# The end of an attention kernel: unit-matrix sums of two steps at a time, and a last block without GpSimd

## What is computed

```python
tgt = concat([target (B,S,64), pos (B,S,2)]) @ proj_w + proj_b
din = concat([tgt, seq, tgt - seq, tgt * seq])          # 256 features
h = sigmoid(din @ w1 + b1)                               # 80 units
h = sigmoid(h @ w2 + b2)                                 # 40 units
score = where(mask == 0, -1e9, h @ w3 + b3)              # (B, S)
attn = softmax(score, axis=-1)
out = einsum('bs,bsd->bd', attn, seq)                    # (512, 64)
```

## Time and profile before

| | us |
|---|---|
| median of 3 runs (lowest, highest) | 285.75 (284.81, 287.69) |
| profiled execution | 287.8 |
| its span in the profile | 286.0 |

### The profile page before, as it was taken

The page is one execution under the profiler, slowest core; times in us unless marked ns, Lnnn a source line. Parts: engine busy times, 40 slices in busy tenths (PEclk is TensorE's granted clock), DMA queues, the critical chain, the costliest instruction groups (busy, mean ns, idle before and its releaser), DMA issues.

```text
span 286.0 us, 5595 instructions
## 1 busy us (share of the span) xinstructions
PE 266.9 (93%) x2132; PEld 86.3 (30%) x2132; DVE 230.7 (81%) x333; ACT 152.0 (53%) x257; POOL 193.8 (68%) x125
## 2 busy tenths in 40 slices
PE   4649999999999999999999999999999999998495
PEld 1313222232232322322323223223232232232194
DVE  3498799799797897997987979979979799757652
ACT  2003267467556664775575647655855485557400
POOL 2000000029989989799799897997998979979480
PEclk9995799999999999999999999999999999999969
DMA  6989999998998997989999999999999990700400
GB/s 118 180 123 200 153 173 311 169 185 301 151 239 230 180 316 137 179 305 146 185 301 174 259 218 171 316 182 188 307 160 305 170 315 1 296 0 0 149 0 18
DMA packets 216750, 53.70 MB, mean 188 GB/s; under 512 B 209556, under 2 KB 210068, under 8 KB 216724
## 3 DMA queue, kind: packets, MB, share of 16 engines
q1 hardware_dynamic: 211640, 52.70, 83.7%
q10 hardware_dynamic: 5084, 0.64, 1.5%
HBM read 53.20 MB, written 0.13 MB: 186 GB/s over the span
## 4 chain that ended last, share of the span: by engine, by line
PE 88%; DVE 5%; SPq 2%; ACT 2%; issue 1%; DMA 1%; ACTq 0%; DVEq 0%
PE pA L415 32%; PE pB L425 16%; PE pL L441 16%; PE pL L448 9%; PE pB L461 7%; PE pL L483 4%; PE pB L471 2%; ACT G L300 1%; DVE X L586 1%; DMA proj_b<-in_L_rec_proj_b 1%; SPq L235 1%; SPq L224 1%; DVE X L595 1%; DVE mix_v L700 1%; DVE HidA L753 0%
## 5 line engine op out<-in xcount | busy, mean ns | idle before, releaser
L564 POOL TENSOR_TENSOR mix<-mix 128x260 f32<-128x260 f32 (+5 forms) x51 | 97.0, 1901 | 5.2 <-POOL acc L557 0.5
L300 ACT ACTIVATE G<-pL,bias 128x512 f32<-128x512 f32 x100 | 60.6, 688 | 69.8 <-PE pL L448 69.8
L291 ACT ACTIVATE HidA<-HidA,VA 128x512 f32<-128x512 f32 x100 | 67.0, 724 | 34.8 <-DVE HidA L753 34.8
L753 DVE TENSOR_TENSOR HidA<-pA,UA 128x1024 f32<-128x1024 f32 x50 | 60.7, 1214 | 24.6 <-PE pA L415 23.9
L553 POOL TENSOR_TENSOR mix<-seq_sb,E 128x4096 f32<-128x4096 f32 (+3 forms) x13 | 77.2, 5941 | 4.1 <-ACT E L321 3.8
L595 DVE SCALAR_TENSOR_TENSOR X<-pT,P_pair,X 128x512 f32<-128x512 f32 x100 | 69.9, 740 | 0.2
L586 DVE STREAM_TRANSPOSE X<-squares 128x1024 f32<-128x1024 f32 x50 | 61.7, 1234 | 0.0
L415 PE MATMUL pA<-X,w_seq 64*64 64x512 f32 x400 | 55.3, 624 | 4.5 <-DVE HidA L753 3.9
L415 PE MATMUL pA<-X,w_sb 64*64 64x512 f32 x400 | 53.5, 606 | 0.0
L551 POOL MEMSET masked<- 128x64 f32 x11 | 1.7, 152 | 73.4 <-ACT E L321 73.4
L425 PE MATMUL pB<-X,wB 128*32 128x512 f32 x400 | 49.8, 617 | 0.0
(11 more groups left out here) (101 smaller groups left out, 118.4 us busy)
## 6 DMA issues: line engine op xcount, KB each, us to landing
squares<-in_L_rec_sequence_emb SPq DMA_DIRECT2D x98, 256.0 KB, 4.7
seq_sb<-in_L_rec_sequence_emb SPq DMA_DIRECT2D x12, 2048.0 KB, 10.0
seq_sb<-in_L_rec_sequence_emb SPq DMA_DIRECT2D x1, 1024.0 KB, 5.0
squares<-in_L_rec_sequence_emb ACTq DMA_DIRECT2D x2, 256.0 KB, 6.0
mask_i<-in_r_mask SPq DMA_DIRECT2D x1, 400.0 KB, 4.7
tgt_sb<-in_L_rec_target_emb SPq DMA_DIRECT2D x1, 128.0 KB, 2.3
out_dram<-result SPq DMA_DIRECT2D x1, 128.0 KB, 2.0
w_sb<-in_L_rec_w ACTq DMA_DIRECT2D x1, 80.0 KB, 3.2
```

The lines of the kernel that those rows point to most:

```text
L291: last = nc.scalar.activation(h, h, ACT.Tanh, scale=0.5, bias=VA[:, 4 * u + i:4 * u + i + 1])
L300: nc.scalar.activation(G[p % NG][:, :], pL2[p % 4][:, :], ACT.Tanh, scale=0.5, bias=bias2[:, 0:1])\
L564: nc.gpsimd.tensor_tensor(mix[:, 0:k, 0:n, :], mix[:, 0:k, 0:n, :], mix[:, 0:k, n:2 * n, :], ALU.add)\
L753: nc.vector.tensor_tensor(HidA[u % NZA][:, :, :], pA[:, :].rearrange("p (i b) -> p i b", i=2), UA[:, :].unsqueeze(1).to_broadcast([P, 2, 5 ...
```

## The change

On VectorE the products of block 10 (`share_products`) are split off from `share_sum`, one quarter at a time; the first is put ahead of `targets_first(49)`. The first half of the products of block 11 is put between the softmax steps of blocks 11 and 12. POOL leaves block 12 out (`KEPT` 0); VectorE multiplies all four quarters of it. On TensorE `layer2_last(23)` goes ahead of `layer1_first(49)`; scores of block 11 go to the second bank of `pA`, and the transposes of blocks 11 and 12 wait only for their rows; `keep_clock(2)` issues two matmuls whose result isn't used; and each matmul of the sums takes two steps side by side, whose two halves VectorE adds at the end. `mix_v[1]`, which block 10's products now use, has 2,048 columns in place of 1,536. The load of block 12 waits for the second part of `share_products`.

```diff
-    KEPT = {SHARED: 2, SHARED + 1: 1, SHARED + 2: 1}
+    KEPT = {SHARED: 2, SHARED + 1: 1, SHARED + 2: 0}
...
         def bank3(c):
-            return pB if c < NBLK - 1 else pL2[0]
+            return {NBLK - 2: pA[:, 512:1024], NBLK - 1: pL2[0]}.get(c, pB)
...
-        shared_bank = {SHARED: pT, SHARED + 1: pA[:, 0:512], SHARED + 2: pA[:, 512:1024]}
+        shared_bank = {SHARED: pT, SHARED + 1: pA[:, 0:512], SHARED + 2: pB}
...
                 if c - RING >= SHARED:
-                    sp.wait_ge(s_part, 1)
+                    sp.wait_ge(s_part, 2)
...
             def transpose_scores(c, groups):
-                pe.wait_ge(s_zb, groups)
-                if c > 0:
-                    pe.wait_ge(s_soft, SOFT * c)
+                if c < NBLK - 2:
+                    pe.wait_ge(s_zb, groups)
+                    if c > 0:
+                        pe.wait_ge(s_soft, SOFT * c)
                 pe.wait_ge(s_rows, c + 1)
...
             def add_products(c, part):
-                n, k = steps_of(c) // 2, Q - KEPT[c]
+                n, k = steps_of(c) // 4, Q - KEPT[c]
                 pe.wait_ge(s_prod, 2 * (c - SHARED - 1) + part + 1)
+                pairs = products_v(c).rearrange("p q (x i) d -> p x q (i d)", i=2)
                 for x in range(n):
-                    last = nc.tensor.matmul(sums[c][:, 0:k * D].rearrange("p (q d) -> p q d", q=k), ident[:, :],
-                                            products_v(c)[:, :, part * n + x, :], start=(part == 0 and x == 0),
+                    last = nc.tensor.matmul(sums[c][:, 0:2 * k * D].rearrange("p (q d) -> p q d", q=k), ident[:, :],
+                                            pairs[:, part * n + x, :, :], start=(part == 0 and x == 0),
                                             stop=(part == 1 and x == n - 1))
...
+            def keep_clock(count):
+                for _ in range(count):
+                    nc.tensor.matmul(sums[NBLK - 1][:, :], ident[:, :], X2[0][:, :], start=True, stop=True)
...
+                if n == NGRP - 1:
+                    layer2_last(g)
                 if n < NGRP:
                     layer1_first(2 * n + 1)
...
-                if 0 <= g < NGRP:
+                if 0 <= g < NGRP and n != NGRP - 1:
                     layer2_last(g)
...
             transpose_scores(NBLK - 2, NGRP)
             transpose_scores(NBLK - 1, NGRP)
+            keep_clock(2)
...
-            for c in range(NBLK):
+            for c in range(NBLK - 1):
                 n = steps_of(c)
                 e = E[c % NE]
...
+            def share_products(c, x):
+                n, q0 = steps_of(c), KEPT[c]
+                k = Q - q0
+                prod = mix_v[1][:, 0:k * D * n].rearrange("p (q d s) -> p q s d", q=k, d=D)
+                dve.wait_ge(s_exp_v, c - SHARED + 1)
+                dve.wait_ge(s_seq[c % RING], 16 * (c // RING + 1))
+                nc.vector.tensor_tensor(prod[:, x:x + 1, :, :], seq_sb[c % RING][:, q0 + x:q0 + x + 1, 0:n, :],
+                                        exp_v(c)[:, x:x + 1, 1:n + 1].unsqueeze(3).to_broadcast([P, 1, n, D]),
+                                        ALU.mult).then_inc(s_part, 1)
...
-                nc.vector.tensor_tensor(acc[:, q0:Q, 0:D], acc[:, q0:Q, 0:D],
-                                        sums[c][:, 0:k * D].rearrange("p (q d) -> p q d", q=k), ALU.add)\
-                  .then_inc(s_last, 1)
+                halves = sums[c][:, 0:2 * k * D].rearrange("p (q i d) -> p i q d", q=k, i=2)
+                for i in range(2):
+                    dve.wait_ge(s_last, done + 2 + 2 * i)
+                    nc.vector.tensor_tensor(acc[:, q0:Q, 0:D], acc[:, q0:Q, 0:D], halves[:, i, :, :], ALU.add)\
+                      .then_inc(s_last, 1)
...
                 if c is not None:
                     softmax_step(c)
+                if n == NGRP - 1:
+                    share_products(SHARED, 0)
...
             targets_last(NGRP - 1)
+            share_products(SHARED, 1)
             share_sum(SHARED)
             softmax_step(NBLK - 2)
+            last_products(NBLK - 2, 0)
             softmax_step(NBLK - 1)
-            last_products(NBLK - 2)
-            last_products(NBLK - 1)
+            last_products(NBLK - 2, 1)
+            last_products(NBLK - 1, 0)
+            last_products(NBLK - 1, 1)
             last_sums(NBLK - 2)
             last_sums(NBLK - 1)
-            dve.wait_ge(s_last, 8)
-            dve.wait_ge(s_sum, NBLK)
+            dve.wait_ge(s_last, 2 * LAST)
```

More of the change, by code:

```diff
@@ L37, in din_attention_program @@
     SHARED = NBLK - 3
-    KEPT = {SHARED: 2, SHARED + 1: 1, SHARED + 2: 1}
-    MOST = Q - min(KEPT.values())
+    KEPT = {SHARED: 2, SHARED + 1: 1, SHARED + 2: 0}
     NEG_INF = -1000000000.0
@@ L133, in din_attention_program @@
         mix = sb("mix", [P, Q, BLK, D + 1])
-        mix_v = [sb("mix_v0", [P, MOST * D * BLK]), sb("mix_v1", [P, MOST * D * BLK // 2])]
+        mix_v = [sb("mix_v0", [P, 3 * D * BLK]), sb("mix_v1", [P, 2 * D * BLK])]
         acc = sb("acc", [P, Q, D + 1])
@@ L147, in bank3 @@
         def bank3(c):
-            return pB if c < NBLK - 1 else pL2[0]
+            return {NBLK - 2: pA[:, 512:1024], NBLK - 1: pL2[0]}.get(c, pB)
         def bank_st(c):
-            return pB if c < NBLK - 1 else pL2[1]
+            return {NBLK - 2: pA[:, 512:1024], NBLK - 1: pL2[1]}.get(c, pB)
         sums = {NBLK - 2: pL2[2], NBLK - 1: pL2[3]}
@@ L196, in din_attention_program @@
         s_out = sem("output_stored")
-        SOFT, PART = 4, 5
+        SOFT, PART, LAST = 4, 6, 5
         TGT_T, W_SET, P_SET, U_SET, B1_SET, V_SET, W2_SET, W3_SET, BIAS_SET = range(1, 10)
@@ L213, in part_v @@
             k = Q - KEPT[c]
-            return shared_bank[c][:, 256:256 + k * (D + 1)].rearrange("p (q d) -> p q d", q=k)
+            return shared_bank[c][:, 128:128 + k * (D + 1)].rearrange("p (q d) -> p q d", q=k)
         def products_v(c):
@@ L318, in exponentials @@
                     nc.scalar.activation(exp_v(c), shifted[c % 2][:, k:Q, 0:w], ACT.Exp).then_inc(s_exp_v, 1)
+                if k == 0:
+                    return
                 if c >= NE:
@@ L452, in layer3 @@
             def layer3(c, groups):
-                pe.wait_ge(s_zb, groups)
-                if 0 < c < NBLK - 1:
-                    pe.wait_ge(s_soft, SOFT * c)
+                if c < NBLK - 2:
+                    pe.wait_ge(s_zb, groups)
+                    if c > 0:
+                        pe.wait_ge(s_soft, SOFT * c)
+                else:
+                    pe.wait_ge(s_za, NQ)
                 pe.wait_ge(s_g, last_pair(c) + 1)
@@ L674, in share_sum @@
                 e, part = exp_v(c), part_v(c)
-                prod = mix_v[0][:, 0:k * D * n].rearrange("p (q d s) -> p q d s", q=k, d=D)
-                dve.wait_ge(s_exp_v, c - SHARED + 1)
-                dve.wait_ge(s_seq[c % RING], 16 * (c // RING + 1))
+                prod = mix_v[1][:, 0:k * D * n].rearrange("p (q d s) -> p q d s", q=k, d=D)
                 dve.wait_ge(s_sum, c)
-                nc.vector.tensor_tensor(prod.rearrange("p q d s -> p q s d"), seq_sb[c % RING][:, q0:Q, 0:n, :],
-                                        e[:, :, 1:n + 1].unsqueeze(3).to_broadcast([P, k, n, D]), ALU.mult)\
-                  .then_inc(s_part, 1)
                 nc.vector.tensor_tensor(acc[:, q0:Q, :], acc[:, q0:Q, :], e[:, :, 0:1].to_broadcast([P, k, D + 1]),
@@ L684, in share_sum, with last_products @@
                 nc.vector.tensor_reduce(part[:, :, D:D + 1], e[:, :, 1:n + 1], AX.X, ALU.add).then_inc(s_part, 1)
-                dve.wait_ge(s_part, 1)
+                dve.wait_ge(s_part, k)
                 nc.vector.tensor_reduce(part[:, :, 0:D], prod, AX.X, ALU.add).then_inc(s_part, 1)
-                dve.wait_ge(s_part, 4)
+                dve.wait_ge(s_part, PART - 1)
                 nc.vector.tensor_tensor(acc[:, q0:Q, :], acc[:, q0:Q, :], part, ALU.add).then_inc(s_part, 1)
-            def last_products(c):
+            def last_products(c, part):
                 n, q0 = steps_of(c), KEPT[c]
@@ L695, in last_products @@
                 dve.wait_ge(s_seq[c % RING], 16 * (c // RING + 1))
-                if c == SHARED + 1:
+                if c == NBLK - 1:
                     dve.wait_ge(s_part, PART)
[L698 to L702, removed]
+                x = slice(part * n // 2, (part + 1) * n // 2)
+                nc.vector.tensor_tensor(products_v(c)[:, :, x, :], seq_sb[c % RING][:, q0:Q, x, :],
+                                        exp_v(c)[:, :, 1 + x.start:1 + x.stop].unsqueeze(3)
+                                        .to_broadcast([P, k, n // 2, D]), ALU.mult).then_inc(s_prod, 1)
             def last_sums(c):
@@ L707, in last_sums @@
                 k = Q - q0
-                done = 4 * (c - SHARED - 1)
+                done = LAST * (c - SHARED - 1)
                 e, part = exp_v(c), part_v(c)
                 if c == SHARED + 1:
-                    dve.wait_ge(s_sum, c)
```

(1 more changed line is left out.)

## The result

Six runs each: median 281.98 us (281.43 to 283.92) against 285.67 (284.73 to 287.69), ratio 0.988, 95% interval 0.984 to 0.992. The change is faster by 1.2%: clear of no change by the interval, and less than 2%. The forecast was 282.6 us, faster, with a range of 281.3 to 285.2. The profiled execution takes 283.9 us, its span 282.1.

What follows compares the result with a forecast made beforehand. Bound at the end by a TensorE-ScalarE ping-pong over the last two groups, then sums partly at half clock. 1.0 + 1.19 + 1.96 - 0.53 = 3.62 us, taken as 3.1: 285.75 to 282.6 us, range 281.3 to 285.2.

Steps and rivals of the forecast that it cites:

- layer 2 in front (to the maximum of block 11): Layer 2 of group 23 ahead of layer1_first(49): ScalarE's tanh come earlier, all behind gains 1.0 us, at most 1.05.
- order and banks (to the first product): Block 12's transposes no longer wait; block 11's first product precedes block 12's softmax step: 1.19 us beside the 1.0.
- sums (first sum to VectorE's addition): TensorE's unit-matrix sums take 8.86 in place of 10.82 us at full clock: 1.96 us less.
- last additions: VectorE's one addition of 192 columns becomes two of 256, 0.46 each: 0.53 us more, between 0.39 and 0.65.
- The clock: TensorE's clock stays full through the sums, with two extra matmuls in a wait; all at half would lose 6.70 us.
- Side by side: Two steps per matmul in the sums: gains nothing by itself, since the column count sets the pace.
- The split: VectorE's block 10 products as two halves of 1.84 us, the first put into a wait: cost 0.
- the step from the profiled execution to the median: Profiled execution is 2.05 us over the median; half a microsecond off the 3.62 leaves a gain of 3.1.
- the rival that the ordinary run of before had little half clock: In the old sums: the gain is then 0.9 to 1.9, about 284.4 us; chance 0.13.
- The other rivals: Clock falls and returns, 284.9 us (0.17); block 10's first half late, 285.85 (0.05); nearly all sums at half clock (0.05).
- the clock did not fall: Rival: clock falls and comes back as before, 5.5 us of sums at half, 2.75 more, 284.9 us; chance 0.17.
- the addition for unit 49 (L775): Rival: VectorE's block 10 first half waits for POOL, this addition starts 3.2 us later, 285.85 us; chance 0.05.

Runs made afterwards that it cites:

- quarters: Block 11's products in four parts, one extra matmul, against changed kernel with one step per matmul and POOL keeping one quarter of block 12: 282.19 us, ratio 0.983.

## Why the prediction was right, and where it was not

By its own steps, from `layer2_first(23)` on:

| step | predicted | measured in the traces | alone, by an experiment |
|---|---|---|---|
| layer 2 in front (to the maximum of block 11) | 1.0 | 14.99 - 14.09 = 0.90 | 0.88 |
| order and banks (to the first product) | 1.19 | 2.25 - 1.05 = 1.20 | order 0.47, banks 0.73 |
| sums (first sum to VectorE's addition) | 1.96 | 10.82 - 8.89 = 1.93 | clock 1.69; 2.72 in the old sums |
| last additions | -0.53 | 1.05 - 1.58 = -0.53 | second addition 0.46 |
| sum | 3.62 | 3.50 | |

The chain from the maximum of block 11 on was the right one, the pace per column held (24 records in 8.86), and each term came within 0.1 us. The last additions came out by some luck: the prediction took the middle of two bounds without a row that decides between them, and the middle, 0.46 each, is what was measured.

Layer 2 was 0.1 short of its term, because another engine ended that stretch than the one that the prediction followed. It reckoned the 1.0 along ScalarE's tanh. In the chain that ended last in the changed kernel, TensorE works through from `layer2_first(23)` to `layer2_last(24)`:

```profile
252.36 1.88 PE pL L442 x16
254.23 1.07 PE pL L449 x8
255.30 1.88 PE pA L416 x16
257.18 1.85 PE pB L426 x16
259.04 1.95 PE pL L442 x16
260.99 1.11 PE pL L449 x8
```

These are 8.63 us of TensorE's own matmuls, where before took 9.52 to the same point (262.19 - 252.67); an earlier tanh could give no more than the difference of 0.89.

- The clock. It stayed full, and the runs without and with the extra matmuls show that these keep it. Without them, with only transposes in the 2.5 us before the sums, it fell at 270.1. The Trainium skill says in "TensorE: Matmul & The Clock Gate", Part 4 (PE-mode transpose), that the full clock does not engage for transposes. The fall agrees with that; but TensorE was also mostly empty there (0.51 us of work in 2.5), so no run here tells the rule from plain idleness.
- Side by side. That it gains nothing by itself was right, and the run shows that it loses 0.39. I priced block 12's fourth quarter as columns and did not set against it that POOL could have kept it for nothing; the run shows 0.98.
- The split costs nothing, as forecast; it also brings nothing.
- What was off is the step from the profiled execution to the median. I put the 2.05 us by which the profiled execution exceeds the median partly on half clock within the sums, and took 0.5 us off the gain. Without that the forecast would have been 285.75 - 3.62 = 282.1, beside 281.98. The traces differ by 2.2 us at the start, as the last section shows, and the profiled execution of before has the longer start; that is enough for the 2.05. No trace of the median run says which start it had. Against the rival that the ordinary run of before had little half clock stand the times beside those of before with the extra matmuls, above.
- The other rivals did not come: the clock did not fall, and the addition for unit 49 (L775) waited for TensorE, 0.78, and not for VectorE.

Two readings of the page's slices are wrong in the prediction: TensorE is at nine tenths from the fourth to the fifth last slice, and towards the end the lower clock shows in the second last slice alone (the earlier trace rows has the clock):

```profile
PE   4649999999999999999999999999999999998495
```

The sums rest on the windows, which are read rightly.

## What to carry to other kernels

Before an end phase that TensorE must run fast, look at the granted clock row by row: an idle stretch ahead of it cost sums of 8 to 9 us another 1.7 to 2.7 here, and one or two matmuls whose result isn't used, put into a wait that is there anyway, bought that back. Where columns set the pace of matmuls, as here, merging them gains next to nothing (0.06 us), and what is merged has to be added up again on VectorE (0.46). Work moved off an engine that had room costs where it lands (0.98). When a wait is taken away, ask which engine ends the stretch next: that sets how much of it is gained. To compare ends, measure from a point that both kernels share, and look at the start of an execution before the spread of medians is explained by the change.

## What the runs showed of the hardware

Executions differ by some 2.2 us in a stretch at the start that no kernel here touched. The window 25 to 31 us, of the changed kernel and of the one with one step a matmul:

```profile
25.00:31.00 6.00, 6.00 (x30) 2.39 (x30) 3.58 (x9) 1.34 (x2) 0.00 (x0) 0.50 0.88 167
```

```profile
25.00:31.00 6.00, 6.00 (x58) 2.35 (x54) 5.59 (x12) 2.06 (x3) 0.00 (x0) 1.00 1.11 202
```

In the first, half clock lasts until 31 us and 30 matmul records fit; in the second it is over by 25 us and 58 fit. Of the eleven traces, four have 30 records there (before, changed, no extra matmuls, quarters) and start `layer2_first(23)` at 252.3 to 252.7; seven have 46 to 58 and start it at 250.1 to 250.6. The records are the surer sign: without the extra matmuls the clock row says 1.00 in this window, though only 30 records fit, as at half clock. Why the clock comes back at one time or the other is open.
